# Moving setup work of the first two chunks from VectorE and ScalarE to GpSimd in a fused layer kernel

## What is computed

```python
r, k, v = sigmoid(x @ Wr.T), x @ Wk.T, x @ Wv.T          # D = 256
state = cumsum(k * v / scale, axis=1) * scale            # scale = sigmoid(decay) ** t, clipped
y = r * state;  y = y * rsqrt(mean(y * y) + 1e-6) * ln_w
x1 = layernorm(x + y @ Wo.T)
h = gelu(x1 @ (alpha1 * sign(w1)).T + b1)                # H = 1024, alpha = mean |w| of each row
out = layernorm(x1 + h @ (alpha2 * sign(w2)).T + b2)
```

## Time and profile before

| | us |
|---|---|
| median of three runs (lowest, highest) | 822.54 (822.36, 822.70) |
| the profiled execution's own time | 822.86 |
| its span, first to last instruction | 821.0 |
| mean granted TensorE clock | 0.998 |
| TensorE busy | 798.2 (97%) |
| VectorE busy | 772.6 (94%) |
| ScalarE busy | 678.9 (83%) |
| GpSimd busy | 295.6 (36%) |

### The profile page before, as it was taken

One profiled execution on the slowest core, in us unless ns is written; L12 is line 12 of the kernel. 1 busy time (PEld: TensorE's weight loads), 2 busy tenths in 40 slices (PEclk: granted clock), 3 DMA queues, 4 the chain that ended last, 5 costly groups with the idle time before them and its releaser, 6 DMA issues.

```text
span 821.0 us, 16564 instructions
## 1 busy us (share of the span) xinstructions
PE 798.2 (97%) x5173; PEld 505.3 (62%) x5173; DVE 772.6 (94%) x1467; ACT 678.9 (83%) x971; POOL 295.6 (36%) x570
## 2 busy tenths in 40 slices
PE   6989999999999999999999999999999999999986
PEld 4555666656666656666656666665666665666653
DVE  7998999999999999999999999999999999999886
ACT  7887888888888888888888888888888888887775
POOL 3343323344323344233344333344332334332344
PEclk9999999999999999999999999999999999999999
DMA  8413554444553434554434554444455344444313
GB/s 249 91 46 78 129 113 94 102 103 102 128 128 83 110 88 102 128 128 92 113 80 109 118 128 103 102 90 108 109 128 112 93 98 106 102 102 103 78 33 97
DMA packets 169847, 86.27 MB, mean 105 GB/s; under 512 B 130145, under 2 KB 165473, under 8 KB 169825
## 3 DMA queue, kind: packets, MB, share of 16 engines
q1 hardware_dynamic: 148304, 52.97, 29.8%
q0 software_dynamic: 4608, 16.78, 10.8%
q10 hardware_dynamic: 16912, 16.26, 5.8%
HBM read 20.45 MB, written 16.78 MB: 45 GB/s over the span
## 4 chain that ended last, share of the span: by engine, by line
PE 89%; DVE 4%; POOL 2%; issue 2%; ACT 2%; DMA 1%; POOLq 0%; DVEq 0%; ACTq 0%; SPq 0%
PE ps_r L362 28%; PE ps_o L483 26%; PE ps_f L433 19%; PE ps_r L433 6%; PE ps_o L388 6%; PE ps_o L393 3%; DVE hid_lo L981 1%; DMA x_in<-in_L_attn_x_dram 1%; DVE u L932 1%; ACT hid L662 1%; DVE u_st L940 0%; PE ps_s L370 0%; POOL root L1284 0%; POOL y_sqs L1272 0%; ACT hid_hi L697 0%
## 5 line engine op out<-in xcount | busy, mean ns | idle before, releaser
L483 PE MATMUL ps_o<-w2T,hid_hi 128*128 128x256 f16 x992 | 218.9, 273 | 3.4 <-DVE hid_lo L981 3.0
L483 PE MATMUL ps_o<-w2T,hid_lo 128*128 128x256 f16 x992 | 218.8, 273 | 0.0
L362 PE MATMUL ps_r<-x_t,proj_hi 128*128 128x512 f16 x768 | 197.1, 379 | 1.7 <-DVE proj_lo L1057 1.2
L433 PE MATMUL ps_f<-x_t,w1T 128*128 128x512 f16 x768 | 181.7, 379 | 1.6 <-DVE x_t L965 1.3
L662 ACT ACTIVATE hid<-ps_f,b1c,f_scale 128x512 f32<-128x512 f32 x192 | 145.3, 774 | 41.6 <-PE ps_f L433 36.6
L981 DVE SCALAR_TENSOR_TENSOR hid_lo<-hid,hid_scale,hid_hi 128x1024 f16<-128x1024 f32 (+1 forms) x136 | 160.3, 1222 | 0.9 <-POOL hid_hi L1305 0.6
L1272 POOL TENSOR_TENSOR y_sqs<-y_sq 128x512 f32<-128x512 f32 x32 | 46.7, 1459 | 308.4 <-ACT y_sq L637 308.4
L362 PEld LDWEIGHTS ps_r<-x_t,proj_hi 128*128 128x128 f16 x768 | 74.5, 98 | 92.1 <-issue 3.4
L697 ACT ACTIVATE hid_hi<-hid,hid_scale 128x2048 f16<-128x2048 f32 (+2 forms) x72 | 128.0, 1778 | 3.2
L433 PEld LDWEIGHTS ps_f<-x_t,w1T 128*128 128x128 f16 x768 | 74.9, 98 | 79.6 <-issue 1.6
L362 PE MATMUL ps_r<-x_t,proj_lo 128*128 128x512 f16 x384 | 114.2, 379 | 0.0
(11 more groups left out here) (182 smaller groups left out, 1333.0 us busy)
## 6 DMA issues: line engine op xcount, KB each, us to landing
x_in<-in_L_attn_x_dram SPq DMA_DIRECT2D x32, 512.0 KB, 4.4
res<-b_row POOLq DMA_DIRECT2D x32, 512.0 KB, 4.6
out_dram<-res ACTq DMA_DIRECT2D x31, 512.0 KB, 3.1
w_in<-in_L_ffn_w_dram SPq DMA_DIRECT2D x2, 1024.0 KB, 10.2
x_t<-x_st SPq DMA_TRANSPOSE x59, 4.3
b_row<-in_L_ffn_b_dram SPq DMA_DIRECT2D x1, 512.0 KB, 13.2
proj_in<-in_L_attn_Wk_dram SPq DMA_DIRECT2D x1, 256.0 KB, 5.2
proj_in<-in_L_attn_Wv_dram SPq DMA_DIRECT2D x1, 256.0 KB, 5.4
```

The lines of the kernel that those rows point to most:

```text
L362: last = nc.tensor.matmul(ps_r[:, m, :], w[:, m, dc, ec * P:(ec + 1) * P], xx[:, :, dc, :], start=(n == 0), stop=(n == 3 * DC - 1))
L433: last = nc.tensor.matmul(f1_bank[hc % NF], w1T[:, hc, dc, :], xx[:, :, dc, :], start=(dc == 0 and n == 0), stop=(dc == DC - 1 and n == 1))
L483: last = nc.tensor.matmul(o_tok[:, tt, :], hh[:, hc, tt * P:(tt + 1) * P], w2T[:, :, hc, :], start=(hc == 0 and n == 0), stop=(hc == HC - ...
```

## The change

GpSimd takes over, in the setup stage only: `norm1` of chunks 0 and 1, the sum of `hid_bound`, the scale `f1_scale`, the scaling of alpha2, one of the two gatings of chunk 1 (two instructions in place of one: a product, then a sum), and the high part of one pair of hidden tiles of chunk 0 (`hh_first`, 1024 columns). Of ScalarE's two alpha2 sums one now stands before the first `gelu`, one between the third and the fourth. VectorE's |b1| moves forward; `x1l_rows(1, 1)` moves behind the fourth `hl`, and `x1h_rows(1, 1)` behind the fourth `hh`. On GpSimd `x1b(0, 0)` now comes after `norm1(1, 0, 1)`; chunk 1's `u_shift` is no longer made. The loop is as before, but for two semaphore counts that are one lower.

```diff
@@ ScalarE
+            def alphas2(dcs):
                 act.wait_ge(s_w2_in, 16)
-                for dc in range(DC):
+                act.wait_ge(s_sgn2, 1)
+                for dc in dcs:
...
                 r_gates(2, 2, (0,))
-                act.wait_ge(s_sgn2, 1)
-                alphas2()
                 x1h(0, 1)
                 ysq(1, (1,), y=y_second)
                 r_gates(2, 2, (1,))
-                act.wait_ge(s_ready, 1)
+                alphas2((0,))
+                act.wait_ge(s_fscale, 1)
                 gelu(0, range(0, 1))
                 yh(1, y_second)
                 gelu(0, range(1, 2))
-                act.wait_ge(s_ready, 2)
+                act.wait_ge(s_ready, 1)
                 hh(0, pairs[0])
-                gelu(0, range(2, 4))
-                hh(0, pairs[1])
-                gelu(0, range(4, 6))
-                hh(0, pairs[2])
+                gelu(0, range(2, 3))
+                alphas2((1,))
+                gelu(0, range(3, 6))
+                hh(0, pairs[2], counted=2)
                 gelu(0, range(6, 8))
+                hh(0, pairs[3])
                 x1h_rows(1, 1)
-                hh(0, pairs[3])
@@ VectorE
+                if by_pool:
+                    dve.sem_inc(s_y, 1)
+                    return
                 dve.wait_ge(s_scan, 2 * c + ec + 1)
                 nc.vector.scalar_tensor_tensor(out=y[:, ec, :], in0=r_tanh[:, ec, :], scalar=1.0,
...
-                scans(1, 1, 0, y_second)
+                scans(1, 1, 0, y_second, by_pool=True)
...
                 kvs(2, 2, 0)
-                norm1(0, 0, 0)
                 scans(1, 1, 1, y_second)
                 hidden_bound()
...
                 kvs(2, 2, 1)
-                norm1(1, 0, 1)
                 hl(0, pairs[1], first=True)
                 hl(0, pairs[2], first=True)
+                hl(0, pairs[3], first=True)
                 x1l_rows(1, 1)
-                hl(0, pairs[3], first=True)
                 scans(2, 2, 1)
@@ GpSimd
+            def norm1(c, b, j):
+                pool.wait_ge(s_urstd, c + 1)
+                pool.wait_ge(s_stored[j], 16 * b + 16)
+                for tt in range(TT):
+                    nc.gpsimd.tensor_scalar(res[j][:, tt, :], u[:, tt, :], u_mv[:, tt, 0:1], u_rstd[:, tt:tt + 1],
+                                            ALU.subtract, ALU.mult).then_inc(s_x1, 1)
+
+            def gated(c, j, ec, y):
...
+                nc.gpsimd.tensor_tensor(y[:, ec, :], r_tanh[:, ec, :], state[j % 2][:, ec, :],
+                                        ALU.mult).then_inc(s_prod, 1)
+                pool.wait_ge(s_prod, 1)
+                nc.gpsimd.tensor_tensor(y[:, ec, :], y[:, ec, :], state[j % 2][:, ec, :],
+                                        ALU.add).then_inc(s_y_pool, 1)
...
                 unscales(2, 2)
+                gated(1, 1, 0, y_second)
                 root_rms(0)
                 root_u(0)
+                norm1(0, 0, 0)
+                hidden_sum()
                 ysqs(1)
...
                 scales(3, 3)
-                diagonal()
                 root_rms(1)
                 unscales(3, 3)
+                diagonal()
+                hh_first(pairs[1])
+                root_u(1)
+                norm1(1, 0, 1)
                 pool.wait_ge(s_b2_in, 16)
                 x1b(0, 0)
-                root_u(1, True)
```

More of the change, by code:

```diff
@@ L692, in norm2, with hh @@
                                          bias=z_shift[:, tt:tt + 1], scale=z_rstd[:, tt:tt + 1]).then_inc(s_zout, 1)
-            def hh(c, part):
+            def hh(c, part, counted=0):
                 act.wait_ge(s_gelu, HC * c + part.stop)
                 nc.scalar.activation(hid_hi[:, part, :], hid[:, part, :], ACT.Copy,
-                                     scale=hid_scale[:, :]).then_inc(s_hh, part.stop - part.start)
+                                     scale=hid_scale[:, :]).then_inc(s_hh, part.stop - part.start + counted)
             act.dma_start(dec_c[:, 0, :], decay.rearrange("(c p) -> p c", p=P),
@@ L944, in ustats @@
                     nc.vector.bn_aggr(u_mv[:, tt, :], u_st[:, tt, :]).then_inc(s_umv, 1)
[L946 to L951, removed]
             def xl_rows(c, j):
@@ L969, in hl @@
             def hl(c, part, tail=None, first=False):
-                if first:
+                if first and part.start == 2:
+                    dve.wait_ge(s_hh_pool, 1)
+                elif first:
                     dve.wait_ge(s_hh, part.stop)
@@ L1118, in hidden_bound @@
             def hidden_bound():
[L1120 to L1124, removed]
+                dve.wait_ge(s_hsum, 1)
                 nc.vector.tensor_reduce(w_max[:, 5:6], hid_bound[:, 1, :], AX.X, ALU.max).then_inc(s_wmax, 1)
-                nc.vector.tensor_scalar_mul(f1_scale[:, :], alpha1[:, :], 1.0 / (D * X1S)).then_inc(s_ready, 1)
             def hidden_scale():
@@ L1272, in ysqs, with hidden_sum, hh_first @@
                 nc.gpsimd.tensor_tensor(y_sqs[:, :], y_sq[:, 0, :], y_sq[:, 1, :], ALU.add).then_inc(s_ysqs, 1)
-            def diagonal():
-                pool.wait_ge(s_hidden, 1)
+            def norm1(c, b, j):
[5 more added lines that the diff above has]
+            def gated(c, j, ec, y):
+                pool.wait_ge(s_scan, 2 * c + ec + 1)
+                pool.wait_ge(s_r, DC * c + ec + 1)
+                nc.gpsimd.tensor_tensor(y[:, ec, :], r_tanh[:, ec, :], state[j % 2][:, ec, :],
[3 more added lines that the diff above has]
+                                        ALU.add).then_inc(s_y_pool, 1)
+            def hidden_sum():
+                pool.wait_ge(s_alpha, HC)
+                pool.wait_ge(s_absb1, 1)
+                nc.gpsimd.tensor_tensor(hid_bound[:, 1, :], hid_bound[:, 0, :], alpha1[:, :], ALU.add).then_inc(s_hsum, 1)
+                nc.gpsimd.tensor_scalar(f1_scale[:, :], alpha1[:, :], 1.0 / (D * X1S), 1.0, ALU.mult,
+                                        ALU.mult).then_inc(s_fscale, 1)
+            def hh_first(part):
+                pool.wait_ge(s_gelu, part.stop)
+                pool.wait_ge(s_ready, 1)
+                nc.gpsimd.tensor_scalar(hid_hi[:, part, :], hid[:, part, :], hid_scale[:, :], 1.0, ALU.mult,
+                                        ALU.mult).then_inc(s_hh_pool, 1)
+            def diagonal():
+                pool.wait_ge(s_alpha, HC + DC)
+                pool.wait_ge(s_hread, 1)
+                nc.gpsimd.tensor_scalar(alpha2[:, :], alpha2[:, :], w_max[:, 5:6], 1.0 / (H * HTOP), ALU.mult,
+                                        ALU.mult).then_inc(s_alpha2, 1)
+                pool.wait_ge(s_alpha2, 1)
                 for dc in range(DC):
```

21 lines of the change are left out of this document (12 added, 9 removed).

## The result

The changed kernel takes **835.21 us** (median of 4 runs, 833.52 to 836.30); the kernel before, measured beside it, 822.45. The ratio is 1.0153, 95% interval 1.0141 to 1.0165. The forecast was 824.1, with a range up to 826.5, so it was right in the sign and 11 us too small, far outside its range. The profiled execution took 835.01 with a span of 833.2, 12.2 us more than the span before.

A forecast was written before the change was run, and what follows sets the result against it. TensorE is busy throughout the loop, so setup edits only move its gapless start. The early +0.6 lies inside the later chains and the later one decides: +1.6 on the median 822.54 gives 824.1 us, range 821.5 to 826.5.

The forecast's parts named there:

- the chain through `hid_lo`: F2 of chunk 0 waits 2.1 us for hid_lo; gaining there is worth at most 1.15 us alone.
- the sign of the sum: Whole kernel: the change was forecast to make it slower, by +1.6 us.
- Price of a norm1 tile: Each 256-column norm1 tile on GpSimd: taken as 0.45 us, between bounds of 0.37 and 0.69.
- step 3: Setup up to chunk 1's statistics: the 0.6 us delay is carried on, u_mv complete at 56.8, hh_first hidden.
- Step 1, the gating: Gating on GpSimd in two instructions, over at 34.9, so chunk 0's root starts 0.3 us late.
- Step 2, norm1 of chunk 0: Chunk 0's tiles wait out VectorE's scan and end at 44.1; x1h starts near 44.5, +0.6 us.
- Step 4, the gain: F2 of chunk 0: TensorE waits 0.7 us for hid_lo instead of 2.1, giving 1.8 us of room.
- Step 5, what is late next: Chunk 1's tiles slip in at hl ends, x1l_rows ends 2.7 us later, F1 starts at 69.95, +1.6 us.
- The DMA of b2: GpSimd's b2 load beside the SP queue's transposes in setup: taken as nothing, upper estimate 0.6 us.
- Rival C: TensorE's clock falls in the stall before F1 of chunk 1: +4.2 us, 826.7; chance 0.13.
- A: The shared port hardly binds, chunk 1's tiles follow 1/std at once: -1.0 to -1.3 us; chance 0.22.
- B: GpSimd keeps the port for chunk 1's four tiles in a row: +1.0 us, 823.5; chance 0.20.

The follow-up runs named there:

- added_mean: The whole change, but GpSimd's norm1 tiles add a negated mean instead of subtracting the mean; 829.32 us, ratio 1.0082.
- second_back: The changed kernel with only chunk 1's four norm1 tiles back on VectorE; 828.53 us, ratio 1.0069.
- both_back: The changed kernel with the norm1 tiles of both chunks back on VectorE; 824.36 us, ratio 1.0024.
- first_back: The changed kernel with only chunk 0's four norm1 tiles back on VectorE; 830.99 us, ratio 1.0102.
- tiles_first: added_mean with VectorE's three hl held until chunk 1's four tiles are written, and x1l_rows and x1h_rows in their old order; 826.13 us, ratio 1.0045.
- both_back_order: both_back with chunk 1's x1l_rows and x1h_rows again ahead of the fourth hl and hh; 823.85 us, ratio 1.0018.
- forms: The changed kernel with GpSimd's eight norm1 tiles given various operations and scalars, output not the reference's; 829.66 us, measured once.
- forms_more: The changed kernel with all eight norm1 tiles as one multiplication, plus eight extra GpSimd test instructions in chunk 0; 836.1 us, measured once.

## Why the prediction was wrong, step by step

**Right:** that an edit here can only move the moment of F1 of chunk 1; that the chain through `hid_lo` had little to give; that x1 of chunk 1, through the DMA, would come last; the sign of the sum.

The forecast had F1 of chunk 1 at 69.95, and it is at 78.65, 8.70 later. Of these, 3.94 us arise up to `x1h` of chunk 0 (48.44 for 44.5), 0.51 from there until `u_mv` of chunk 1 is complete (61.25 for 56.8), 3.31 from there to the end of the last tile (70.86 for 63.1), and 0.94 from there to F1. The clock's 1.98 us come on top.

**Price of a norm1 tile: the step that failed most.** I took 0.45, bounded by 0.37 and 0.69 from rows of `diag` and `hid_hi`. Those rows are multiplications. The tile subtracts, and costs 1.21. The bounds went by columns and by nothing else; the operation was the one thing in which no row of the trace was near. With the cheap operation it is 0.55, inside my bounds. At seven tiles, 1.21 for 0.45 is 5.3 us; 1.21 for 0.55, what `added_mean` changed, is 4.6, and it shows 5.9. In the profiled executions, which lie 5.5 apart, it can be placed: `x1h` of chunk 0 begins 2.24 us sooner (46.20 for 48.44); from there to `u_mv` of chunk 1 it is 11.90 us for 12.43, for the clock stays at 1.00 there and does not in the changed kernel (step 3); and from `u_mv` to the end of the four tiles it is 7.33 for 9.99. So the tiles themselves are 4.9 and a fall of the clock 0.5.

The Trainium skill ("GPSIMD Engine Reference", Engine selection) says that one-input work on GpSimd runs at roughly line rate. These runs agree roughly for mult and add (0.40 to 0.55 us a tile; VectorE needs 0.35) and contradict it for subtract and max in `tensor_scalar`, at 1.06 to 1.21.

**Step 1, the gating:** +0.3 forecast, +1.1 measured. I had `y_lo` win the port. GpSimd's product starts 0.3 us before it, and the second instruction got in ahead of |b1| as well. Its worth is 1.2 us of the median.

**Step 2, norm1 of chunk 0:** `x1h` at 48.44, +4.5 instead of +0.6. The mechanism held (the scan keeps the first tile out until 43.25, the other three run freely), the gating's 1.1 came on top, and each tile's 1.21.

**Step 3:** `hh_first` took 1.12 us and is hidden, as said. `u_mv` of chunk 1 is late by 5.06 (60.87 against 55.81), which is the 4.5 handed on and some half a microsecond more. I had no fall of the clock here. Behind TensorE's waits for the tiles (0.24, 0.77, 0.76 and 0.76 us) the granted clock was 0.50 from 48.5 to 52 us:

```profile
49.00:50.00 1.00, 1.00 (x3) 0.30 (x2) 0.50 (x1) 1.00 (x3) 0.00 (x0) 0.50 0.00 0
```

From `x1h` of chunk 0 to `u_mv` of chunk 1 it is 12.43 us here, 12.74 in `second_back`, whose clock is low for longer, and 11.90 in `both_back` and `added_mean`, whose clock is 1.00 from 46 to 54 us. So the half microsecond is the clock's.

**Step 4, the gain:** as forecast. The waits of TensorE for `hid_lo` in the setup fall from 2.1 us to 0.2, and buy nothing.

**Step 5, what is late next:** right in its chain, wrong in how tiles get in. I had one tile slip in at the end of each `hl`. In the changed kernel none did. The size was then 8.01 us for four tiles instead of 4.8, on top of a start 4.5 us late.

**The DMA of b2, which I took at nothing.** Queue of SP in the changed kernel and in `both_back`:

```profile
73.40 5.37 SPq L295 DMA_TRANSPOSE x_t<-x_st  x2
```

```profile
65.34 5.06 SPq L295 DMA_TRANSPOSE x_t<-x_st  x2
```

From there to F1 it is 5.25 us in the changed kernel, 5.22 in `added_mean` and 5.45 in `first_back`, where b2's DMA is issued 2.6 us ahead of the first transpose. It is 4.61 in `both_back` and 4.60 in `second_back`, where it is issued 6.4 us ahead. So the term was about 0.6 us, the upper bound that I had given it; no run moves this DMA alone.

**Rival C happened with the forecast, not in its place.** I gave it 0.13, as its condition was a stall of near 4 us and I had 3.4. The condition hung on the same tile price as the forecast, so its chance should have gone up with every doubt about that price. Its price, 2.6 us from the first transposes, came out at 1.98. A and B are out: the port did bind, and not by keeping VectorE out.

Where 12.6 of the 12.8 us are, by medians: 5.9 the subtraction, 0.5 of it by the clock; 3.2 the wait for three `hl`, with the clock behind the long stall and the order of `x1l_rows`; 1.2 the gating. The other 2.3 (826.13 - 822.65 - 1.2) are what `tiles_first` has over `both_back_order`, in which VectorE does the tiles. By the rows of the two, one half arises before `x1h` of chunk 0, which begins at 46.20 instead of 45.02 (the first tile waits out the scan), the other from `u_mv` of chunk 1 to F1, 13.80 us for 12.63, where the `hl` wait for the tiles and F2 for the `hl`. No run separates them further. No version here beats the kernel before by what can be measured. The order of `hl`, `kvs` and x1 within VectorE's setup was not varied further.

## What to carry to other kernels

Price a moved instruction by a row with the same operation and not only the same engine and width; where no row has it, widen the bound by the worst ratio between operations that you have seen, or rewrite it into one that you have priced (add a negated mean). When the work moves to an engine that shares a port, look at which side issues first: a queue of back-to-back wide instructions can hold the other out to its end, and letting the short side go first, even with the long side idle, may win. And a rival whose condition is a long stall is not independent of the forecast that makes the stall.

## What the runs showed of the hardware that was not expected

- GpSimd's `tensor_scalar` on 256 f32 columns: add and mult with constants 0.40 us, with two per-partition scalars 0.55; with a subtraction 1.10 to 1.21, whatever the scalars, and with max, which ran with constants only, 1.06. `tensor_tensor` on the same columns takes 0.71 for subtract and for add. Why is not shown.
- How long a waiting GpSimd instruction is kept out by three `hl` in a row is not fixed. In the changed kernel, `first_back` and `added_mean` it waited for all three. In `forms` it got in after the first of them and ended at 61.95, and the three `hl` together took 4.03 us instead of 3.67:

```profile
60.33 4.03 DVE L983 SCALAR_TENSOR_TENSOR hid_lo<-hid,hid_scale,hid_hi 128x1024 f16<-128x1024 f32 x3
```

  In `forms_more` it took 2.55 us and got in after the second (L1274; the highest duration is chunk 1's first tile, the last start its second):

```profile
L1274 POOL TENSOR_SCALAR res<-u,u_rstd x4: 885/1400/2547, 42.2 to 69.5; 128x256 f32<-128x256 f32 x4
```

  The starts of tile and first `hl` lay 0.2 to 0.4 us apart in all of them. What decides stays open. The Trainium skill ("SBUF — State Buffer", SBUF: two separate sides) says that whichever starts first has the port for its whole instruction and the other blocks. The first wait of each row agrees; which of the two is next in line it does not say.
- TensorE's granted clock fell to 0.50 (1.2 GHz) not only behind stalls of 5.04, 7.73 and 7.95 us, at a cost of 1.9 to 2.1 us each, but also behind one of 2.44 us in `tiles_first`, and behind four waits of 0.2 to 0.8 us for chunk 0's tiles in the changed kernel and in `second_back`. Behind 1.33 us in `both_back` it did not. In `tiles_first` and in the changed kernel the short cases show the fall only after work had resumed, in `second_back` already between the waits. Rival C was tied to a stall of near 4 us, after the one fall at the end of the run; these falls lay outside its condition.
